# The last query tile's scores brought forward and its probabilities turned by DMA, in an attention and feed-forward block

## The reference

```python
x = x + attn(layernorm(x), W_qk, W_v, alibi_slope)     # one head, causal, width 128
x = x + ffn(layernorm(x), w_gate, w_up, w_down)        # int weights, hidden width 384
# attn: scores = (x @ W_qk) @ x.T * 128**-0.5 + (kpos - qpos) * slope, masked above the diagonal
#       softmax(scores) @ (x @ W_v.T)
# ffn:  h = silu(x @ wg.T) * (x @ wu.T);  h @ wd.T
```

## Time and profile before

| | us |
|---|---|
| median of 3 executions | 143.63 |
| lowest, highest | 143.48, 143.95 |
| the profiled execution's own time | 143.12 |
| its span in the trace | 141.1 |

### The profile page before, as it was taken

How to read it: one execution, slowest core, us unless ns; L and a number is a source line. 1 busy time by engine, 2 the same in 40 slices (tenths; PEclk the granted TensorE clock), 3 DMA queues, 4 the chain that set the end, 5 groups by cost and what they waited for, 6 DMA issues and landing times.

```text
span 141.1 us, 3405 instructions
## 1 busy us (share of the span) xinstructions
PE 119.1 (84%) x1183; PEld 88.1 (62%) x1183; DVE 119.3 (85%) x336; ACT 109.4 (78%) x249; POOL 103.4 (73%) x162
## 2 busy tenths in 40 slices
PE   0278578999999999889999998988994789979961
PEld 0066164768987869777869975667842545656661
DVE  0759989998788995989987969998869999998892
ACT  4035779999966999757999949977869689988920
POOL 6491789964992545996895999479669999995810
PEclk9999999999999999999999999999999999999999
DMA  4896000000000000000000001643001303057625
GB/s 133 230 255 177 3 2 2 5 2 0 5 0 0 5 0 2 0 5 0 0 5 0 5 0 40 99 89 79 0 5 37 79 0 79 6 73 213 198 78 153
DMA packets 18515, 7.28 MB, mean 52 GB/s; under 512 B 9152, under 2 KB 18496, under 8 KB 18496
## 3 DMA queue, kind: packets, MB, share of 16 engines
q1 hardware_dynamic: 18496, 7.02, 20.6%
HBM read 2.82 MB, written 2.10 MB: 35 GB/s over the span
## 4 chain that ended last, share of the span: by engine, by line
PE 32%; DVE 27%; POOL 14%; ACT 13%; DMA 5%; issue 5%; SPq 2%; DVEq 0%; POOLq 0%
DVE probsT_lo L805 5%; POOL hidden_lo L411 5%; PE work_ps L553 5%; PE attn_ps L566 3%; DVE biased L822 3%; DVE stats L707 3%; PE score_ps L501 3%; PE score_ps L503 3%; DMA x2T_lo<-xn_lo 3%; PE attn_ps L568 3%; PE attn_ps L567 3%; PE score_ps L502 3%; ACT probs L960 3%; ACT probsT_hi L982 2%; DVE xs L832 2%
## 5 line engine op out<-in xcount | busy, mean ns | idle before, releaser
L566 PE MATMUL attn_ps<-v_hi,probsT_hi 128*128 128x128 f16 x144 | 25.8, 219 | 2.4 <-DVE xs L832 1.7
L805 DVE TENSOR_TENSOR probsT_lo<-work_ps,probsT_hi 128x512 f16<-128x512 f32 (+3 forms) x48 | 25.2, 553 | 3.0 <-ACT probsT_hi L982 2.7
L960 ACT ACTIVATE probs<-biased,neg_max 128x128 f32<-128x128 f32 (+7 forms) x32 | 25.0, 783 | 3.2 <-DVE neg_max L822 3.1
L982 ACT CAST probsT_hi<-work_ps 128x512 f16<-128x512 f32 (+3 forms) x48 | 21.4, 483 | 6.4 <-PE work_ps L553 6.2
L822 DVE CUSTOM_DVE_ANT_0 biased<-score_ps,bias,neg_score_scale 128x128 f32<-128x128 f32 (+7 forms) x32 | 25.8, 806 | 0.6 <-PE score_ps L503 0.6
L568 PE MATMUL attn_ps<-v_hi,probsT_lo 128*128 128x128 f16 x144 | 25.8, 219 | 0.0
L567 PE MATMUL attn_ps<-v_lo,probsT_hi 128*128 128x128 f16 x144 | 25.7, 219 | 0.0
L553 PE MATMUL work_ps<-ident,probs 128*128 128x128 f32 x144 | 21.4, 274 | 1.3 <-DVE probsT_lo L805 0.7
L707 DVE BATCH_NORM_STATS2 stats<-xs 128x6 f32<-128x128 f32 x64 | 15.2, 283 | 5.2 <-DMA xs<-in_L_attn_x_dram 3.7
L553 PEld LDWEIGHTS work_ps<-ident,probs 128*128 128x128 f32 x144 | 16.5, 141 | 4.4 <-DVE probsT_lo L805 1.0
L566 PEld LDWEIGHTS attn_ps<-v_hi,probsT_hi 128*128 128x128 f16 x144 | 14.1, 98 | 5.5 <-DVE probsT_lo L805 1.8
(11 more groups left out here) (138 smaller groups left out, 331.5 us busy)
## 6 DMA issues: line engine op xcount, KB each, us to landing
out_dram<-xs SPq DMA_DIRECT2D x7, 256.0 KB, 3.2
xs<-in_L_attn_x_dram SPq DMA_DIRECT2D x3, 512.0 KB, 8.2
xs<-in_L_attn_x_dram SPq DMA_DIRECT2D x2, 256.0 KB, 3.1
out_dram<-xs SPq DMA_DIRECT2D x2, 128.0 KB, 2.0
wgu_int<-in_L_ffn_w_gate_dram SPq DMA_DIRECT2D x1, 192.0 KB, 3.0
wgu_int<-in_L_ffn_w_up_dram SPq DMA_DIRECT2D x1, 192.0 KB, 3.1
wd_int<-in_L_ffn_w_down_dram SPq DMA_DIRECT2D x1, 192.0 KB, 3.5
x2T_hi<-xn_hi SPq DMA_TRANSPOSE x8, 2.5
```

Source lines behind the costliest of these rows:

```text
L566: pe.matmul(attn_ps[:, 0:D], p_hi, v_j, start=(j == 0), stop=False)
L805: dve.tensor_tensor(probsT_lo[:, i % 2, cols], work_ps[:, bank, 0:n], probsT_hi[:, i % 2, cols], ALU.subtract).then_inc(work_emptied, 1)
L960: act.activation(probs[:, i % 2, 0:n], biased[:, i % 2, 0:n], ACT.Exp, bias=neg_max[:, i:i + 1], scale=-1.0, accum_out=prob_sum[:, i:i + 1 ...
L982: act.copy(probsT_hi[:, i % 2, CW * h:CW * h + n], work_ps[:, bank, 0:n]).then_inc(probsT_hi_ready, 1)
```

## The change

`LONG = 7` names the last tile. Its path through the rounds becomes another:

- Its scores stand behind round 0's last work on TensorE (before: at the start of round 4); the bias on VectorE is the first of round 1; the exponentials on ScalarE stand in round 1 between the copy of tile 2's turned probabilities and the preparation's part. A list `score_order` (0, 1, 2, 3, 7, 4, 5, 6) now numbers the scores, and the buffers go by place in it.
- TensorE no longer turns its probabilities. They lie in SBUF as `long_probs`; ScalarE casts them to float16 in two halves in rounds 2 and 3, VectorE subtracts in two halves after the additions of rounds 3 and 4, and SP turns the four pieces of a batch by DMA. Its two fills leave the ring.
- SP's queue: the DMA transposes of batches 0 to 2 stand ahead of all of the FFN's, those of batch 3 between the FFN's first four and its next four.
- VectorE's reciprocal no longer waits for the scores and probabilities that its next instruction needs; these waits stand with that instruction. Statistics number 4 have a buffer of their own.
- `EARLY = 3`: the three gate and up blocks of chunk 0 stand in rounds 5, 6 and 7 of the last batch, the two blocks of hidden values that VectorE makes there in rounds 6 and 7, the load of ScalarE's table for silu in round 5 (before: round 7).

The diff, cut to its core:

```diff
-    EARLY = 2
+    EARLY = 3
...
+    LONG = TB - 1
+    score_order = [0, 1, 2, 3, LONG] + list(range(4, LONG))
+
+    def place(b, i):
+
+        return TB * b + score_order.index(i)
...
-            if nb < B:
+            if nb < B and ni != LONG:
                 ring += [("P", nb, ni, h) for h in range(ni // CT + 1)]
...
+            def turn_long(b):
+                if b:
+
+                    sp.wait_ge(attn_ready, TB * b)
+                for h in range(HALVES):
+                    for part, ready, o in ((long_hi, long_hi_ready, longT_hi), (long_lo, long_lo_ready, longT_lo)):
+                        sp.wait_ge(ready, HALVES * b + h + 1)
+                        sp.dma_start_transpose(o[:, CT * h:CT * (h + 1), :], part[:, CW * h:CW * (h + 1)])\
+                          .then_inc(longT_landed, 16)
+
+            for b in range(B - 1):
+                turn_long(b)
             for n in range(B, NROUND):
+                if n == B + 1:
+                    turn_long(B - 1)
...
             def weigh_values(b, par, i):
-                taken(("P", b, i, i // CT))
+                if i == LONG:
+                    pe.wait_ge(longT_landed, 64 * (b + 1))
+                else:
+                    taken(("P", b, i, i // CT))
...
             def around(b, par, nxt, final):
                 for i in range(TB):
-                    if i + 3 < TB:
+                    if i + 3 < LONG:
                         scores(b, par, i + 3)
-                    elif not final:
+                    elif i + 3 >= TB and not final:
                         scores(b + 1, nxt, i + 3 - TB)
...
-                        pe.wait_ge(biased_ready, NT - EARLY + 1 + j)
+                            pe.wait_ge(biased_ready, NT)
+                        if j == HB - 1:
+                            pe.wait_ge(work_emptied, VECTOR_TAKES)
                         gate_up(0, 0, [j])
                     weigh_values(b, par, i)
+                    if i == 0:
+                        scores(b, par, LONG)
...
-                if j == 0 and n not in (0, 1, B + 3):
-                    dve.wait_ge(pool_step, steps_before(n) - N_STEPS + N_READ)
+                if j == 0 and n not in (0, 1, B, B + 3):
+                    dve.wait_ge(pool_step, steps_before(n - 1 if n == B + 1 else n) - N_STEPS + N_READ)
...
+            def long_low(b, h):
+                cols = slice(CW * h, CW * h + CW)
+                dve.wait_ge(long_hi_ready, HALVES * b + h + 1)
+                if b:
+                    dve.wait_ge(longT_landed, 64 * b)
+                dve.tensor_tensor(long_lo[:, cols], long_probs[:, cols], long_hi[:, cols], ALU.subtract)\
+                   .then_inc(long_lo_ready, 1)
...
                 for i in range(TB):
-                    more = i + 3 < TB or not final
-                    inverse_sum(b, i, more)
-                    if more:
-                        bias_scores((i + 3) % TB)
+                    inverse_sum(b, i)
+                    if i == 1:
+                        bias_scores(b, LONG)
+                    if i + 3 < LONG:
+                        bias_scores(b, i + 3)
...
                     add_attention(b, i)
+                    if i in (3, 4):
+                        long_low(b, i - 3)
...
+            def long_high(b, h):
+                cols = slice(CW * h, CW * h + CW)
+                act.wait_ge(probs_ready, place(b, LONG) + 1)
+                if b:
+                    act.wait_ge(longT_landed, 64 * b)
+                act.copy(long_hi[:, cols], long_probs[:, cols]).then_inc(long_hi_ready, 1)
...
+                    if final and i >= TB - EARLY:
+                        silus(0, 0, [i - (TB - EARLY)])
+                    if i == 1:
+                        exponentials(b, LONG)
+                    if i in (2, 3):
+                        long_high(b, i - 2)
                     for part in parts_at(b, i):
                         copy_high(b + 1, nxt, *part)
```

More of the change, by code:

```diff
@@ L83, in by_pool, with copied_probs @@
         return key[0] in ("xT", "q") and key[1] > 0
+    def copied_probs(key):
+        return sum(k[0] == "P" for k in ring[:ring_index[key] + 1])
     def emptied(key):
@@ L170, in preln_block @@
         probsT_lo = sb("probsT_lo", [P, 2, S], F16)
+        long_probs = sb("long_probs", [P, S], F32)
+        long_hi = sb("long_hi", [P, S], F16)
+        long_lo = sb("long_lo", [P, S], F16)
+        longT_hi = sb("longT_hi", [P, TB, P], F16)
+        longT_lo = sb("longT_lo", [P, TB, P], F16)
         neg_max = sb("neg_max", [P, TB], F32)
@@ L532, in scores @@
             def scores(b, par, i):
-                t = TB * b + i
+                t = place(b, i)
                 if i in (0, 2):
@@ L542, in scores @@
                     keys = slice(k0, min(k0 + CW, P * (i + 1)))
-                    m = three(score_ps[:, i % 2, keys], (at(qT_hi, par, rows), at(qT_lo, par, rows)),
+                    m = three(score_ps[:, buf, keys], (at(qT_hi, par, rows), at(qT_lo, par, rows)),
                               (at(xT_hi, par, keys), at(xT_lo, par, keys)))
@@ L683, in _ @@
             for c in range(NCH):
-                gate_up(c, c % 2, range(EARLY if c == 0 else 0, HB))
+                if c:
+                    gate_up(c, c % 2)
                 if c >= LAG:
@@ L851, in around @@
                 for i in range(TB):
-                    more = i + 3 < TB or not final
-                    inverse_sum(b, i, more)
-                    if more:
-                        bias_scores((i + 3) % TB)
-                    if i + 1 < TB:
+                    inverse_sum(b, i)
[3 more added lines that the diff above has]
+                        bias_scores(b, i + 3)
+                    elif i + 3 >= TB and not final:
+                        bias_scores(b + 1, i + 3 - TB)
+                    if i + 1 < LONG:
                         split_probsT(b, i + 1)
-                    elif not final:
+                    elif i == LONG and not final:
                         split_probsT(b + 1, 0)
@@ L868, in around @@
                             statistics(b + 4, i - 1)
-                    if final and i == TB - 1:
-                        multiply(0, range(EARLY))
+                    if final and i > TB - EARLY:
+                        multiply(0, [i - (TB - EARLY) - 1])
                     add_attention(b, i)
+                    if i in (3, 4):
+                        long_low(b, i - 3)
                     for n, k in statistics_at(b, i):
@@ L932, in _ @@
             for c in range(NCH):
-                multiply(c, range(EARLY if c == 0 else 0, HB))
+                multiply(c, range(HB - 1 if c == 0 else 0, HB))
                 if c >= LAG:
@@ L982, in copy_probsT, with silus @@
                     act.copy(probsT_hi[:, i % 2, CW * h:CW * h + n], work_ps[:, bank, 0:n]).then_inc(probsT_hi_ready, 1)
+            def silus(c, par, blocks=range(HB)):
+                for j in blocks:
+                    act.wait_ge(gate_up_ready, HB * c + j + 1)
+                    act.activation(silu[:, par, j, :], gate_ps[j], ACT.Silu, scale=gate_scale[:, 0:1])\
+                       .then_inc(silu_ready, 1)
             def around(b, par, nxt, final):
@@ L1036, in _ @@
             around(B - 1, (B - 1) % 2, B % 2, True)
-            def silus(c, par, blocks=range(HB)):
-                for j in blocks:
-                    act.wait_ge(gate_up_ready, HB * c + j + 1)
-                    act.activation(silu[:, par, j, :], gate_ps[j], ACT.Silu, scale=gate_scale[:, 0:1])\
-                       .then_inc(silu_ready, 1)
             def hidden_high(c, blocks=range(HB)):
```

77 lines of the change are left out of this document (42 added, 35 removed).

## The result

The changed kernel takes 150.23 us (median of four runs, 149.23 to 150.96); the kernel before took 143.56 us on the same chip (four runs, 143.4 to 143.95). The ratio is 1.0456, with an interval of 1.0391 to 1.0521: **4.6% slower**, 6.7 us by the medians. Forecast were 148.3 us and a range up to 150.6. In the table further down the medians and ranges are of all executions of a kernel, while its ratio leaves out one slow execution each of e1, e2, e6 and e10 (over 1.5% above the fastest of the same kernel), so it need not be the quotient of the medians. The profiled execution took 150.36 us with a span of 148.3 us, which is 7.2 us more than the span of before.

A forecast was written before the change was run, and what follows sets the result against it. ScalarE's back-to-back work up to the last `whole` copy was taken as the bound. Batch terms summed to 3.3 to 5.5 us, taken as 4.7: 147.8 on the profiled execution, 148.3 as a median, range 145.6 to 150.6.

The forecast's parts named there:

- Step 1: Round 0: tile 7's scores delay ScalarE's tile 2 copy by 1.12 us (t0: TensorE begins tile 3's scores in round 0).
- Steps 2 and 3: ScalarE, rounds 1 to 3: exponential 7 ahead of the `whole` copies adds 1.13 us, two casts of `long_probs` 1.04.
- The cover of 0.74: ScalarE's last `whole` copy of q is 0.74 us ahead of TensorE's first v part; no other cover.
- The ring's wait: TensorE waits at q and v for ScalarE's `whole` copies, since each part takes the bank the last part left.
- Step 4: Behind the first v part: tile 7's transposes (1.07 us) and 0.37 of waits go, leaving TensorE's own 5.78 of 7.22.
- Batch 0: Keeps its starting wait for the first turned probabilities; given batch 2's difference, +1.3 to +1.8 us.
- Batch 1: Same 21.3 to 21.85 us as batch 2; its 1.51 wait for GpSimd's statistics reads goes: +0.2 to +0.8.
- Batch 3: No `whole` copies; VectorE's later chain, less tile 7's transposes, copies and subtractions, plus third gate block: +0.5 to +1.1 us.
- rival C: DMA transposes land late, at 4.0 us each, and TensorE waits in batch 3's round 7: up to 2 us, 150.3; 5 in 100.
- Behind the rounds: The chain there is GpSimd's and starts with the last addition: 0 counted, a gain of at most 0.9 us.
- B (VectorE and GpSimd in each other's way): New two-SBUF-input subtractions contend with GpSimd, 0.85 us more in each batch: 8.1 in all, 151.7 us; 14 in 100.
- A (ScalarE absorbs it): TensorE sets the pace, its 1.44 us relief shows in three batches, batch 1's 1.51 wait goes: 137.8 us; 9 in 100.

The follow-up runs named there:

- e1: Changed kernel with tile 7's scores, bias, exponential, casts and subtractions one round later: 153.76 us, ratio 1.0663 to the kernel before.
- e2: Changed kernel without the casts of `long_probs` and their subtractions, exponential 7 written straight as float16 (tile 7's rows inexact): 145.28 us, ratio 1.0114.
- e6: Changed kernel with exponential 7 behind round 1's two `whole` copies instead of ahead of them: 151.07 us, ratio 1.0477.
- e10: Changed kernel with the casts of `long_probs` on GpSimd in batches 0 to 2, batch 3's still on ScalarE: 147.24 us, ratio 1.0218.
- e7: Changed kernel with early scores and exponential 7 kept, but TensorE turning tile 7's probabilities as before, no casts or DMA in the attention: 148.22 us, ratio 1.0288.
- e3: Changed kernel with each cast of `long_probs` made twice, the first into a buffer nobody reads: 154.92 us, ratio 1.0742.
- e8: Changed kernel with tile 7's scores from the high parts alone, one matmul where three stood (less exact): 150.07 us, ratio 1.0425.
- e9: Changed kernel with statistics number 4 back in the shared buffer, with its wait as before: 151.91 us, ratio 1.0553.
- e5: Changed kernel with `EARLY` back at 2, the third gate block behind the rounds: 149.94 us, ratio 1.0424.
- e4: Kernel before with only the third statistics buffer added: 143.04 us, ratio 0.9943.

## Why the prediction was right, and where its sizes were off

**The direction and the mechanism held.** Step by step, in batch 2:

- *Step 1, the hole.* Forecast: the copy of tile 2 at t0+3.65. Measured: t0+3.68. The experiment with one matmul in three made the hole smaller by 0.52 and the batch by 0.44 (in batch 1 by 0.54 and 0.07, as a wait for VectorE's bias came in its place).
- *Steps 2 and 3, exponential 7 and the casts.* Forecast: ScalarE has no slack and gives way at t0+15.35. Measured: t0+15.21. Doubling the casts put all of their 1.04 on each batch, and taking them to GpSimd took 1.04 off.
- *The cover of 0.74.* The forecast had the first v part at t0+15.5, straight behind the `whole` copy. It came at t0+15.82. The wait ahead of tile 6's transposes ended not with ScalarE's copy but with VectorE's subtraction `probsT_lo` of tile 5, 0.60 us. The ring's wait that TensorE meets is more often VectorE's (5.9 us in 11 waits over the whole kernel) than for ScalarE's `whole` (1.6 us in three): VectorE's subtraction runs behind ScalarE's copy of the same bank, so ScalarE's lateness reaches TensorE through it.
- *Step 4, what is left behind v.* Forecast between 5.78 (TensorE's own work) and 6.35 (through VectorE's chain). Measured: 6.31, near the upper end, but that is in part luck. What stood there before, less the transposes, is 7.22 - 1.07 = 6.15. The lower end also took off 0.37 of waits: the one wait there, 0.18 before, did not go, and is 0.20 in the changed kernel. Together with the late v this makes 22.13 where the forecast's ends were 21.3 and 21.85.
- *Batch 0.* Forecast +1.3 to +1.8, measured +1.51.
- *Batch 1.* Forecast +0.2 to +0.8, measured +1.05. It was taken to be as long as batch 2, without the wait, and so it was (sharing the buffer again costs 1.63). So the term that was too small is again the length of a batch, 22.13.
- *Batch 3.* Forecast +0.5 to +1.1, measured +1.64. The third gate block is 0.39 to 0.40 of it and the late landing of 4.33 us 0.24, which the forecast had only as rival C. The terms that the forecast names for this batch, 1.5 to 2.2 less 1.07 plus 0.87, make 1.3 to 2.0. They come down to its +0.5 to +1.1 only by taking off tile 7's copies and subtractions too, and no run shows that these counted there. The early scores with their exponential are not small there either: e7, without casts or DMA, still took 20.11, 1.08 over before, with the third block in it.
- *Behind the rounds.* Forecast 0, measured +0.05.

The sum of the batches was forecast as 3.3 to 5.5, taken at 4.7, and came out as 6.31: batches 1, 2 and 3 were 0.25, 0.31 and 0.54 us over their upper ends, batch 0 within its range. The sum's own ends gave 146.9 to 149.1 us, so 150.23 lies above them, and inside the stated range only because that was widened to 150.6 for rivals C and B, of which only C was seen to cost anything, 0.24 us. The step that was mis-sized is the length of a batch with preparation, taken between 21.3 and 21.85 with VectorE's chain made of rows at their shortest: it measured 22.13 in batches 1 and 2. The last 0.84 us of the 7.2 are the start, which differs between executions of any of these kernels.

**The rivals.** *A (ScalarE absorbs it)* is excluded: ScalarE's stretch ends 3.15 us later, and 1.04 us of work more or less on it moves a batch by 1.03 to 1.04 (by 1.40 where VectorE's subtractions went with it). *B (VectorE and GpSimd in each other's way)* is there in batches 0 to 2, but the price falls on GpSimd, which has room. Three views of the changed kernel follow: all of VectorE's new subtractions (ns, min/median/max); VectorE and GpSimd where the second one of batch 2 runs; GpSimd and VectorE where the first one runs. The fourth is GpSimd in e7, which has no such subtractions, at the place of the second.

```profile
L875 DVE TENSOR_TENSOR long_lo<-long_probs,long_hi x8: 681/682/1101, 34.7 to 103.1; 128x512 f16<-128x512 f32 x8
```

```profile
82.10 0.68 DVE L875 TENSOR_TENSOR long_lo<-long_probs,long_hi 128x512 f16<-128x512 f32 x1
...
82.20 1.60 POOL L474 TENSOR_TENSOR qT_lo<-whole,qT_hi 128x512 f16<-128x512 f32 x1 [1.47 <-ACT whole L1007]
```

```profile
77.14 2.03 POOL L418 TENSOR_TENSOR centred<-xs,mean 128x512 f32<-128x512 f32 x2
...
78.62 1.10 DVE L875 TENSOR_TENSOR long_lo<-long_probs,long_hi 128x512 f16<-128x512 f32 x1
...
79.26 1.48 POOL L474 TENSOR_TENSOR qT_lo<-whole,qT_hi 128x512 f16<-128x512 f32 x1
```

```profile
80.47 1.16 POOL L470 TENSOR_TENSOR qT_lo<-whole,qT_hi 128x512 f16<-128x512 f32 x1 [1.38 <-ACT whole L996]
```

VectorE begins 0.10 us ahead of GpSimd and takes its 0.68, and GpSimd's subtraction takes 1.60 in place of 1.16. This happens at the same place in batches 0, 1 and 2; in e7 all twelve of GpSimd's subtractions take 1.16 or 1.17. Once GpSimd was already at work, on `centred`, and then VectorE was the one that paid: 1.10 in place of 0.68. A third meeting is GpSimd's next subtraction, at 79.26, which took 1.48 (last row of the third view). So a meeting costs 0.32 to 0.44 us, about half of B's 0.85 at the most, and whoever comes second pays it. The first comer had 0.58, 0.55 and 0.46 us left to run when the second began (by the starts and lengths above), so the second lost most of that rest, and never more than it. The meeting that fell on VectorE is in batch 2, which is as long as batch 1, where VectorE met none (22.13), so it cost the batch nothing. The Trainium skill, "SBUF — State Buffer", section "Who interferes with whom", says that a VectorE instruction with two SBUF inputs contends with a GpSimd instruction that reads SBUF, and that the order of issue decides who is blocked. The trace agrees on both. What the forecast's rival had wrong is on whom it would fall. The total of 150.23 lies near B's 151.7 and C's 150.3, and by the total alone one could have taken either for true. *C (the DMA lands late)* cost 0.24 us in one batch. It is real with a round less of time: e1 waited 4.8 us for it.

## What to carry to other kernels

Before work is brought forward, look for the engine that has no gap in that stretch, whatever its share of the whole: ScalarE was busy for 78% of the span before, and yet two casts of 0.52 us in its back-to-back stretch cost their full time in every batch, and nothing on GpSimd. A matmul moved ahead of a transpose delays not itself but whatever reads the transposes. When a change bundles edits, time each alone: the one that helped here, a third buffer for the statistics, was hidden by the others. And when a run is shorter or longer than expected, look whether a DMA landed late in one of the two before putting the difference down to the edit.

## What the runs showed of the hardware

**The clock behind the rounds.** In the changed kernel's profile the granted clock was 1.00 throughout. In the profiles of e1, e3, e7, e8 and e9 it fell for a slice some 14 us behind the rounds, and in e5 at the very end; in those of before, e2, e4, e6 and e10 it didn't. Here is e8 by stretches of 2 us, and one of its matmuls:

```profile
core 0: us, PE busy (x) PEld busy (x) DVE busy (x) ACT busy (x) POOL busy (x), PEclk, DMA share, GB/s
...
122.00:124.00 2.00, 2.00 (x24) 1.45 (x21) 0.66 (x1) 0.53 (x2) 2.00 (x3) 0.70 0.04 9
124.00:126.00 2.00, 2.00 (x6) 0.71 (x5) 1.68 (x3) 0.69 (x1) 2.00 (x2) 0.50 0.60 122
126.00:128.00 2.00, 2.00 (x20) 1.31 (x19) 1.23 (x2) 1.26 (x2) 2.00 (x3) 0.95 0.00 0
```

```profile
124.38 0.63 PE L639 MATMUL score_ps<-x2T_lo,wguT 128*128 128x512 f16 x1
```

0.50 is the lower level, 1.2 GHz of 2.4. The matmuls there start 0.43 us apart (123.10, 123.52, 123.95, 124.38) in place of 0.22, and from the last addition to the end the profile has 39.7 us, not 38.5. Counted so, the six profiles with full clock throughout took 38.2 to 38.9 us, and the five with the fall 39.4 to 40.8. TensorE had been idle before it; here is what ended that idle time in e8, and the same place in the changed kernel, where the clock did not fall.

```profile
121.61 0.23 PE L726 MATMUL work_ps<-wdT,hidden_hi 128*128 128x128 f16 x1 [1.96 <-POOL hidden_lo L449]
```

```profile
122.84 0.23 PE L722 MATMUL work_ps<-wdT,hidden_hi 128*128 128x128 f16 x1 [1.95 <-POOL hidden_lo L449]
```

The idle times are alike, so this pause alone doesn't decide it, and what does stays open. The fall is part of the spread: the changed kernel's four executions span 1.7 us, and the longest, 150.96, is the one whose mean clock was 0.989; those of before span 0.55.

**The DMA transposes** of `long_lo` landed after 2.3 us in the median and after 4.3 at the most, much as those of `x2T_lo` did before (2.5 and 4.0). Their issue on SyncE took 1.19 us, and 2.31 at the most.
